# GpSimd's order of work in the second 8-wide attention stage of a four-layer kernel

## The reference

```python
x = x + L0_xattn(layernorm(x), ctx)          # 16 heads, 8 wide
x = x + L0_ffn(layernorm(x))
x = x + L1_xattn(layernorm(x), ctx, mask)    # linear attention
x = x + L1_ffn(layernorm(x))                 # experts choose tokens
x = x + L2_xattn(layernorm(x), ctx, mask)    # 16 heads, 8 wide  <- the stage that is changed
x = x + L2_ffn(layernorm(x))                 # gated experts, 2 of 8 by distance
x = x + L3_xattn(layernorm(x), ctx)          # 16 heads, 64 wide
x = x + L3_ffn(layernorm(x))
```

```python
dist = sqrt(max(|x|^2 + |c|^2 - 2 x c, 1e-12));  w, sel = top_k(dist, 2);  w = softmax(w)
out = sum over e in sel of  w_e * ((silu(x Wg_e + bg_e) * (x W1_e + b1_e)) W2_e + b2_e)
```

## Time and profile before

| | us |
|---|---|
| plain runs, median of three | 2169.64 |
| profiled execution, its time | 2179.81 |
| profiled execution, its span | 2178.1 |
| PE busy in it | 1791.6 (82%) |
| POOL busy in it | 666.3 (31%) |
| mean granted clock of TensorE | 0.883 |
| first 8-wide stage | 0 to 286 |
| second 8-wide stage | 921 to 1353 |
| gated experts begin | 1353.5 |

### The profile page before, as it was taken

The page is one execution under the profiler, slowest core; times in us unless marked ns, Lnnn a source line. Parts: engine busy times, 40 slices in busy tenths (PEclk is TensorE's granted clock), DMA queues, the critical chain, the costliest instruction groups (busy, mean ns, idle before and its releaser), DMA issues.

```text
span 2178.1 us, 48570 instructions
## 1 busy us (share of the span) xinstructions
PE 1791.6 (82%) x18884; PEld 1276.6 (59%) x18884; DVE 1077.5 (49%) x3087; ACT 911.6 (42%) x2496; POOL 666.3 (31%) x664
## 2 busy tenths in 40 slices
PE   6999974876599999888888473499639999999988
PEld 3556563664477778744544243499616666666763
DVE  5666555675411121234455233466545555555557
ACT  2333311765154444322222111266626555565635
POOL 3322103675011011022111433455432333333315
PEclk8999976887599999978988677699869999999979
DMA  5000001000000000062100000122310000000001
GB/s 163 12 7 7 2 1 29 16 6 3 4 2 2 2 2 2 11 264 95 70 7 2 21 21 21 43 59 58 94 65 6 6 6 6 6 6 1 2 1 39
DMA packets 48830, 63.59 MB, mean 29 GB/s; under 512 B 8106, under 2 KB 37701, under 8 KB 48349
## 3 DMA queue, kind: packets, MB, share of 16 engines
q1 hardware_dynamic: 44253, 51.98, 7.5%
q0 software_dynamic: 4352, 8.47, 1.2%
HBM read 32.29 MB, written 28.65 MB: 28 GB/s over the span
## 4 chain that ended last, share of the span: by engine, by line
PE 54%; issue 10%; DVE 7%; POOL 6%; POOLq 4%; DVEq 2%; DMA 1%; ACT 1%; another core or an unknown queue 1%; SPq 1%; ACTq 0%
PE single L1778 5%; PE quad L1766 5%; PE single L2076 2%; PE quad L2059 2%; PE quad L2065 2%; PE pair L568 2%; PE single L619 2%; PE pair L2434 2%; POOL tokens_by_expert L415 2%; PE pair L1725 2%; PE quad L2434 2%; PE single L2446 2%; POOLq L132 1%; PE quad L2411 1%; PE quad L596 1%
## 5 line engine op out<-in xcount | busy, mean ns | idle before, releaser
L766 DVE TENSOR_REDUCE arena<-pair 128x8 f32<-128x1024 f32 x128 | 156.7, 1224 | 147.0 <-PE pair L568 145.1
L2667 POOL TENSOR_TENSOR arena<-arena 128x512 f32<-128x512 f32 x128 | 130.5, 1042 | 312.7 <-DVE arena L2590 312.7
L890 POOL TENSOR_SCALAR arena<-arena 128x512 f32<-128x512 f32 x56 | 86.8, 1566 | 367.1 <-ACT arena L688 367.1
L262 POOL TENSOR_TENSOR rstd<-var_eps,neg_half 128x4 f32<-128x4 f32 (+1 forms) x64 | 68.4, 1069 | 342.3 <-DVE var_eps L258 242.8
L744 ACT ACTIVATE arena<-quad 128x1024 f32<-128x1024 f32 x128 | 124.1, 1021 | 78.5 <-PE quad L602 78.5
L568 PE MATMUL pair<-arena 32*128 32x512 f32 x512 | 153.5, 673 | 0.0
L1836 ACT ACTIVATE arena<-quad,arena 128x256 f32<-128x256 f32 x256 | 110.7, 476 | 100.4 <-PE quad L1766 100.4
L2527 ACT ACTIVATE arena<-pair,arena 128x128 f32<-128x128 f32 x256 | 91.0, 380 | 90.9 <-DVE arena L2585 90.9
L1919 DVE TENSOR_TENSOR arena<-single,arena 128x512 f32<-128x512 f32 x32 | 22.1, 692 | 212.8 <-PE single L1778 212.8
L1766 PE MATMUL quad<-arena,wide 128*128 128x256 f32 x512 | 121.7, 385 | 4.8 <-issue 4.0
L1778 PE MATMUL single<-wide,arena 128*64 128x128 f32 x2048 | 123.9, 275 | 0.0
(11 more groups left out here) (493 smaller groups left out, 4413.8 us busy)
## 6 DMA issues: line engine op xcount, KB each, us to landing
tokens_by_expert<-arena SPq DMA_DIRECT2D x22, 780.0 KB, 8.8
arena<-in_ctxT SPq DMA_DIRECT2D x32, 256.0 KB, 2.8
arena<-tokens_by_expert SPq DMA_DIRECT2D x72, 65.0 KB, 1.9
wide<-in_w SPq DMA_DIRECT2D x2, 2048.0 KB, 9.8
arena<-outputs_by_choice SPq DMA_DIRECT2D x16, 256.0 KB, 5.3
wide<-in_wgu SPq DMA_DIRECT2D x1, 2736.0 KB
x<-in_x SPq DMA_DIRECT2D x4, 512.0 KB, 7.8
out_x<-x SPq DMA_DIRECT2D x8, 256.0 KB, 2.3
```

Source lines behind the costliest of these rows:

```text
L766: dve.tensor_reduce(mx[m % 2][:, 8 * p:8 * p + 8], S[:].rearrange("p (h k) -> p h k", h=8), AX.X, ALU.max).then_inc(s["s_free"], 1)
L890: mm = pool.tensor_scalar(kv[g % 2][:, :, a, :], kf[g % 2], kmask[:, a:a + 1], None, ALU.mult)
L2667: pool.tensor_tensor(part, part, inv[t % 3][:, 4 * r:4 * r + 4].unsqueeze(2).broadcast_to([P, 4, P]), ALU.mult).then_inc(s["norm_ready"], 1)
```

## The change

GpSimd's program in the second 8-wide stage is written anew. `scatter` takes a half: eight transfers for four samples instead of sixteen for eight. For l = 0 the loop is what it was. For l = 2 a turn g is now: the masked keys of g + 2; in turns 3 to 6 a half of unit 0 or 1, after its rows are ready; the bias of group g + 2; and last the deviation of group g itself, where it was that of group g - 2, ahead of the masked keys. Unit 2's sixteen transfers leave the stage's end and stand in `gated_experts` behind GpSimd's tables, ahead of the wait for the last unit's rows.

```diff
--- before.py
+++ after.py
@@ -409,8 +409,9 @@
             dve.tensor_copy(where_i[:, :, mine], where)
             return dve.drain()
 
-        def scatter(pool, k):
-            for n in range(k * UNIT, k * UNIT + UNIT):
+        def scatter(pool, k, half):
+            first = k * UNIT + half * G
+            for n in range(first, first + G):
                 for i in range(2):
                     pool.indirect_dma_start(by_tile, bass.IndirectOffsetOnAxis(ap=where_i[:, i, n:n + 1], axis=0),
                                             xr[:, n, :], None).then_inc(routed, 16)
@@ -923,32 +924,37 @@
                     pool.drain()
                     pool.memset(blank[:, :, P], FAR)
                     pool.drain().then_inc(blanked, 1)
-                for g in range(NG):
-                    if l == 0 and g + 2 < NG:
-                        first_rstd(pool, g + 2)
-                    if l == 0 and g == 2:
-                        later_consts(pool)
-                    if g == 2 and l == 2:
-                        clear_twins(pool, "pipelines", "experts")
-                    if g >= 2:
-                        residual(g)
-                        pool.wait_ge(s["stats_ready"], g - 1)
-                        mm = rstd_of(pool, (g - 2) * G)
-                        if l == 2:
-                            mm.then_inc(s["rstd_ready"], 1)
-                    if g + 2 < NG:
-                        masked(g + 2)
-                    if l == 2 and g in (5, 7):
-                        pool.wait_ge(s["rows_ready"], (g - 3) // 2)
-                        if g == 5:
+                if l == 0:
+                    for g in range(NG):
+                        if g + 2 < NG:
+                            first_rstd(pool, g + 2)
+                        if g == 2:
+                            later_consts(pool)
+                        if g >= 2:
+                            residual(g)
+                            pool.wait_ge(s["stats_ready"], g - 1)
+                            rstd_of(pool, (g - 2) * G)
+                        if g + 2 < NG:
+                            masked(g + 2)
+                    for g in (NG - 2, NG - 1):
+                        pool.wait_ge(s["stats_ready"], g + 1)
+                        rstd_of(pool, g * G)
+                else:
+                    for g in range(NG):
+                        if g + 2 < NG:
+                            masked(g + 2)
+                        if g == 2:
+                            clear_twins(pool, "pipelines", "experts")
+                        if g == 3:
                             pool.wait_ge(blanked, 1 + 16 * FILLS)
-                        scatter(pool, (g - 5) // 2)
-                for g in (NG - 2, NG - 1):
-                    pool.wait_ge(s["stats_ready"], g + 1)
-                    rstd_of(pool, g * G)
-                if l == 2:
-                    pool.wait_ge(s["rows_ready"], 3)
-                    scatter(pool, 2)
+                        if 3 <= g < 7:
+                            k = (g - 3) // 2
+                            pool.wait_ge(s["rows_ready"], k + 1)
+                            scatter(pool, k, (g - 3) % 2)
+                        if g + 2 < NG:
+                            residual(g + 2)
+                        pool.wait_ge(s["stats_ready"], g + 1)
+                        rstd_of(pool, g * G).then_inc(s["rstd_ready"], 1)
                 barrier(pool, phase)
 
             return sync, tensor, scalar, vector, gpsimd
@@ -2258,8 +2264,11 @@
                 pool.iota(steps[:, TILES:TILES + B], pattern=[[P, B]], base=0, channel_multiplier=0)
                 pool.iota(lane, pattern=[[1, 1]], base=0, channel_multiplier=1)
                 pool.drain().then_inc(fw_in[2], 16)
+                for half_unit in range(2):
+                    scatter(pool, K - 1, half_unit)
                 pool.wait_ge(s["rows_ready"], 1)
-                scatter(pool, K)
+                for half_unit in range(2):
+                    scatter(pool, K, half_unit)
 
                 def root(i):
                     part = slice(i * B // 4, (i + 1) * B // 4)
```

## The result

The plain runs took 2082.18 us in the median (2078.66 to 2093.43, four runs) against 2169.68 for the kernel before (2168.87 to 2174.63): a ratio of **0.9601, interval 0.9559 to 0.9643**, or 87.5 us less. 2100 was forecast, within 2053 to 2126. The profiled execution took 2078.66, with a span of 2076.9.

The account below looks back on a forecast made before the run. Late deviations on GpSimd, transfer bursts and half clock were taken to bound the second 8-wide stage. 94.6 saved - 44 for halves + 19 in the tail = 69.6 us off 2169.64, so 2100 us, range 2053 to 2126.

Parts of the forecast that it names:

- What bounds the kernel now: Second 8-wide stage: late deviations, two transfer bursts and half clock leave it 121.6 us longer than the TensorE-bound first.
- The half clock: TensorE in the second 8-wide stage: some 36 us of work at half speed, costing 18 us, 3 per stall.
- the 94.55 of the waits: Second 8-wide stage: 75.2 us of deviation waits plus 19.35 of one burst, a second way to 94.6 of stalls and half clock.
- The deviation ahead of the masked keys: GpSimd's turn, second 8-wide stage: five waits go, later work keeps its cover; 94.6 us are stalls and half clock.
- the routing's work: Second 8-wide stage: work that stays on top of the first stage's, 27 us of the 121.6.
- The halves: Eight transfers per turn in turns 3 to 6, beside busy TensorE: 11 us lost each, 44 in all, bounds 0 to 52.
- The third unit's burst: Sixteen transfers moved from the stage's end to the gated stage: start 24.1 us earlier, less 5.1, gain 19 us.
- A: Rival, not the chip: halves in the second 8-wide stage hold TensorE for their length; 2100 us, 2082 to 2117, chance 0.50.
- B: Rival, not the chip: short bursts are absorbed or the hold is the profiled execution's alone; 2056 or 2076 us, chance 0.34.
- Rival C: GpSimd's turn: a new wait replaces the old, deviation late again; 57 of 94.6 us given back, 2113 to 2130, chance 0.08.
- Rival D: Transfers beside a busy VectorE grow and hold TensorE, making it slower than before: 2216 us, or 2258; chance 0.03.
- What would show it: Profile signs: `rstd` waits at most 1 us, masked-key spacing, reciprocal idle times, stage clock, first tile's load near 45 us.

Follow-up runs that it names:

- 16-row: Changed kernel with its 32 in-stage transfers at 16 of 128 rows, all 48 full ones in the gated stage: 2077.57 us on chip B, 2079.33 on C.
- spaced kernels: Changed kernel with a small power behind each transfer of a half, so 2.3 us apart: 2044.35 us on chip B, 2044.96 on C.

## Why the prediction was right, and where its sizes were off

*What bounds the kernel now* held. With the order alone changed, 72.4 us of the 121.6 between the two stages went; the hold of a burst is real on chip A and lies in the stage's other time. The half clock was too small in it: from 1016.3 to 1328, the ruler before, TensorE is busy for 220.2 us, against 193.2 in the kernel without transfers, for the same 3537 matmuls. So slower matmuls cost 27 us and idle time 78.6, not 18 and the rest. That the 94.55 of the waits agreed with the 94.6 was chance: both were 11 us short.

*The deviation ahead of the masked keys* did what the working says: no wait of `rows_normal` for `rstd` is left in the stage, and GpSimd's turn kept its cover. Rival C falls. Its bounds were of the right kind, but the time left to TensorE was **mis-sized**. I put the routing's work at 27 us; without any transfer the stage takes 206.05 - 190.4 = 15.7 more than the first. From masked keys to masked keys that kernel takes 33.50, 34.82, 33.50 and 35.14 us against 31.55: 1.95 more where my items (2.2 + 1.05) give 3.25, and 3.3 to 3.6 more in a group with a choice of experts, where they give 5.75. The rest, from 1158.76 to the last deviation, takes 69.1 against 286.04 - 221.87 = 64.2. So each kind of group costs some 60% of what I counted; I had added whole durations, as if TensorE had no idle time to put them in. Which of the items is the smaller one was not separated. So 105.9 us were stalls and half clock, not 94.6: 11.3 more. (Most of these rows come from chip A, those of before from the chip of the result.)

*The halves* were forecast at 11 us each, from a lower bound of 0 and an upper of 13. They cost 8.3 in the mean, the last 11.0. The term that was **mis-sized** is the 2 us that TensorE was to work on before it has to stop. In the first three bursts it worked at its pace for 7.2, 7.7 and 8.9 us, and they cost 6.8, 6.8 and 8.5; in the last it worked for 2.4, and that one cost the 11.0 that were forecast. In all it is 10.8 us less lost. The parts were off too, in opposite directions: per burst 3.4 us idle where I had 7.7, and 4.9 of slower matmuls where I had 3. Why the last burst stops TensorE so much sooner isn't shown.

*The third unit's burst* was forecast at 19 and gave 14.1 to 14.3. Two terms are off. The stage starts 3.75 us behind the last deviation's start and not 1.1 (its own length), so 21.5 us earlier, not 24.1. And the tile load moves by 7.4 in the stage and not 5.1; on C, 5.3. The last transfer is issued 5.2 later, as worked out. The other 2.1 lie between it and the load, which takes 5.5 us where it took 3.4 before and takes 3.5 on C. ScalarE's copy of 114x432 numbers waits 35.74 us in that burst, and 22.62 on C.

The sum is then 105.9 - 33.2 + 14.1 = 86.8 against the 69.6 of the forecast. Two of the three errors pointed the same way, and the third took off 4.9, so 2082 lies at the lower end of the range that A had for itself (whose upper end is 2118 by its own terms, not 2117).

*Rivals.* Of A and B, each holds, on its own chip, which I had not thought of: I took the hold for a trait of the kernel or of the profiled execution. That A came out was thus luck of the chip: on C the same kernel takes 2041.06 us, below the whole range, though before is 27 us faster there too, and its gain of 101.9 would be inside. On C by B's rule: 105.9 saved, 21.5 - 5.3 = 16.2 in the tail, less the 19.35 us of the earlier trace rows that before doesn't lose there either, gives 102.7; 101.9 were measured. That before has no hold on B and C was not looked at in a trace of it and is worked out only; its times there are 30 to 32 us below those on A, of which the hold and its half clock explain some 22. The rule of the Trainium skill, "SBUF — State Buffer", section "Who interferes with whom", that "DMA never contends with a compute engine" agrees with the traces of B and C; those with the hold disagree with it, by 33.2 us, though they don't show where the delay arises. Rival D falls: transfers beside a busy VectorE take 0.96 us. The factor of five that the Trainium skill has in "A bandwidth-pool intuition that's wrong (but worth ruling out)", same page, doesn't show in these rows; no run here sets a transfer beside a long VectorE copy, which is its case.

*What would show it:* the masked keys came 33.5 and 34.8 apart, just under the forecast 35 to 38, and 40.3 to 41.9 with a burst, not 46 to 48. The reciprocals wait less often than forecast, three times for 15.7 us in all, because the hold also falls on ScalarE. The clock of 0.92 to 0.93 lies above the 0.85 to 0.9 of A. The gated stage begins its transfers 2.5 us in, and not 1.7, and loads the first tile at 47.4, not near 45.

**What stays open:** what makes TensorE be held on one chip and not on another, and whether it is the rows, the spacing or the length of a burst that does it. A run of the 16-row and the spaced kernels on chip A would tell the second. All executions here were recorded ones (each lists its clock), so none tells how a run without a recorder goes.

## What to carry to other kernels

Look at an in-order engine whose work is small (GpSimd is busy for a third of this span) for a short instruction that others wait for behind long ones that nobody needs yet: 1 us of powers, moved ahead of 8.5 us, was worth 71 of the 87 us (on chip A). Size what is left after such a wait by a stretch that has the same work and no stall, and price the added work only where the bounding engine has no time left for it. Repeat the changed kernel itself as a control beside its variants, on the same chip: it was the one run that separated a cure from a different chip.

## What the runs showed of the hardware

**A burst of indirect transfers from GpSimd can hold TensorE's signals, on some chips.** The ruler of the same kernel is 239.2 us on one chip and 206.0 on another; 206.05 is what it takes with no transfer in the stage. Where there is a hold, it costs 16.7 us for sixteen transfers, 8.3 for eight and 2.2 for four, and 4.9 of the 8.3 are matmuls that run slower, mostly behind the burst at half clock. Each chip stands for one set of runs, so a trait of the chip and one of the time aren't told apart.

**A barrier behind such transfers is longer.** From the last pow's start to the next stage it takes 3.8 us on all three chips (4.2 with four transfers right before the last deviation), even where the last transfer was issued 42 us earlier (1210.35 against 1252.22), also with 16 rows a transfer, and 1.2 in the two kernels that issued none in the stage (on A and B). The timeline of the kernel with no transfer, whose last deviation starts at 1227.85:

```profile
1229.03 0.15 POOL L2258 MEMSET arena<- 128x64 f32 x1 [0.17 <-POOLq L132]
```

**Chips differ by more than the smaller part of the change**, the 14.3 us of the tail. The kernel before takes 2173 us on A and 2141 on B, and the changed one 2082 on the chip of the result and 2041 on C. What a run on one chip shows of a small gain has to be set beside its control on that chip.
